# A four-layer graph network on one core: weights in order of use, a new weaving of the engines' work, and filler products on TensorE

## The reference, cut to what matters

```
L0 (twice): u = h h^T / sqrt(D); a = softmax(u) * adj; attn = a / sum(a)
            ctx = (attn*upper) (h Wl) + diag(attn) (h Ws) + (attn*lower) (h Wr); h = relu(layernorm(ctx))
L1 (twice): u = h (h Wleft)^T, h (h Wright)^T by triangle; attn = exp(u)*adj / sum
            h = relu(layernorm(attn (h Wlin)))
L2:         12 heads: softmax(q k^T * scale + 2 adj) v, then Wo
L3:         12 heads: softmax over edges (q k^T / sqrt(32) + beta adj) v
```

## Time and profile before

| | |
|---|---|
| median of three runs | 3139.33 us (3137.36 to 3139.83) |
| profiled execution | 3139.59 us, span 3137.8 us (1.8 us lie around it) |
| PE busy | 97% of the span |
| DVE, ACT, POOL busy | 83%, 67%, 12% |
| products on PE | 34944, or 546 for a graph |

### The profile page before, as it was taken

How to read it: one execution, slowest core, us unless ns; L and a number is a source line. 1 busy time by engine, 2 the same in 40 slices (tenths; PEclk the granted TensorE clock), 3 DMA queues, 4 the chain that set the end, 5 groups by cost and what they waited for, 6 DMA issues and landing times. The chain is left out here.

```text
span 3137.8 us, 87682 instructions
## 1 busy us (share of the span) xinstructions
PE 3032.1 (97%) x34944; PEld 2337.5 (74%) x34944; DVE 2606.3 (83%) x7641; ACT 2094.4 (67%) x6037; POOL 377.2 (12%) x652
## 2 busy tenths in 40 slices
PE   3899999999999999999999999999999999999986
PEld 1677777777777777777777777777777777777764
DVE  4688888888888888888888888888888888888874
ACT  4467677677677677677676676676676666666664
POOL 1111111111111111111111111111111111111100
PEclk7999999999999999999999999999999999999996
DMA  5000000000000000000000000000000000000000
GB/s 174 4 14 11 10 13 11 12 12 11 13 10 11 13 10 11 13 10 11 13 10 11 14 10 11 13 10 11 14 10 11 13 10 11 14 10 11 10 7 6
DMA packets 37904, 47.82 MB, mean 15 GB/s; under 512 B 4542, under 2 KB 37498, under 8 KB 37498
## 3 DMA queue, kind: packets, MB, share of 16 engines
q1 hardware_dynamic: 31408, 33.31, 3.4%
q10 hardware_dynamic: 6090, 8.91, 0.9%
HBM read 29.59 MB, written 12.58 MB: 13 GB/s over the span
## 5 line engine op out<-in xcount | busy, mean ns | idle before, releaser
L638 ACT ACTIVATE prob<-score,neg_head_max 128x128 f32<-128x128 f32 x1536 | 494.1, 392 | 117.5 <-DVE neg_head_max L901 117.2
L284 PE MATMUL bank_c<-htc_hi,w_hi 128*128 128x128 f16 x2304 | 397.2, 220 | 0.0
L284 PE MATMUL bank_c<-htc_lo,w_hi 128*128 128x128 f16 x2304 | 397.1, 219 | 0.0
L284 PE MATMUL bank_c<-htc_hi,w_lo 128*128 128x128 f16 x2304 | 397.0, 219 | 0.0
L284 PE MATMUL bank_a<-w_hi,hta_hi 128*128 128x384 f16 x1152 | 379.6, 330 | 0.0
L284 PE MATMUL bank_a<-w_lo,hta_hi 128*128 128x384 f16 x1152 | 378.8, 329 | 0.0
L699 DVE SCALAR_TENSOR_TENSOR pt_lo<-bank_c,pt_hi 128x384 f16<-128x384 f32 x512 | 271.1, 550 | 74.3 <-ACT pt_hi L518 70.1
L896 DVE SCALAR_TENSOR_TENSOR score<-bank_c,bias 128x384 f32<-128x384 f32 x512 | 281.0, 549 | 33.7 <-PE bank_c L459 29.8
L901 DVE TENSOR_REDUCE neg_head_max<-score 128x3 f32<-128x384 f32 x512 | 280.4, 548 | 6.8
L518 ACT ACTIVATE pt_hi<-bank_c 128x384 f16<-128x384 f32 x512 | 233.0, 481 | 63.5 <-PE bank_c L328 63.5
L328 PE MATMUL bank_c<-ident,prob 128*128 128x128 f32 x1536 | 257.8, 278 | 14.1 <-ACT prob L638 13.7
(11 more groups left out here) (200 smaller groups left out, 9183.0 us busy)
## 6 DMA issues: line engine op xcount, KB each, us to landing
x_in<-x SPq DMA_DIRECT2D x64, 192.0 KB, 2.4
out<-y_out SPq DMA_DIRECT2D x64, 192.0 KB, 1.9
w_stage<-w_t ACTq DMA_DIRECT2D x8, 576.0 KB, 3.9
adj_in<-adj SPq DMA_DIRECT2D x64, 64.0 KB, 2.1
score<-w_t ACTq DMA_DIRECT2D x4, 576.0 KB, 4.0
prob<-w_t ACTq DMA_DIRECT2D x3, 576.0 KB, 4.0
norms<-norm_rows SPq DMA_DIRECT2D x8, 192.0 KB, 6.3
w_stage<-w_t SPq DMA_DIRECT2D x2, 576.0 KB, 6.3
```

The lines of the kernel that those rows point to most:

```text
L284: mm = nc.tensor.matmul(out_ap, a, b, start=first and i == 0, stop=last and i == len(pairs_of) - 1)
L638: ex = nc.scalar.activation(prob[:, j, c, :], score[:, j, c, :], ACT.Exp, bias=neg_head_max[:, j, c:c + 1])
```

## The change

1. The order of the weights on the host, and with it W_INDEX's inner order, follows their use: L0 left, right, self (before: left, self, right); L2 v, q, k, Wo; L3 v, q, k. `weights` is called for each weight where it is first used, and no longer for a later one of the layer at once.
2. ACT and DVE split no weight ahead of the weaving; all 19 splits stand in SPLITS, which has new places. ACT issues no load of weights and of `bias_hl` any more: SP does, in one written order, with the wait for DVE's split on SP. The norms come in between, the first two early; `qk_bias` is loaded after all weights, ahead of `load(2)`.
3. POOL sets `bias_hl` to zero after the masks.
4. ORDER and FIRST are new for every engine. Each string holds each letter as often as before. Most of the difference is where the period is cut; beside it steps change places with neighbours: on PE `c12` now stands between `w2` and `w3`, with `w4` behind `x0` and only two steps x (before four, a2 and w4) between it and `c13`.
5. PE runs filler products of `ones2` with itself, 128x128, into c3 or a1 (`idle`): 110 ahead of its first step, 211 at eleven places of periods 0 to 2 (WARM_FIRST), and 500 at 37 places of the last three periods (WARM_LAST), which count from the period `graphs`. The results are not used.

The diff, without the renaming on the host, the moved `weights` calls of L1, and the semaphore declarations:

```diff
@@ -13,28 +13,40 @@
 MASKED = -9.0e15
 W_INDEX = (0, 3, 6, 9, 12, 16)
 W_STAGES = 4
-W_FIRST = 3
 
 
 ORDER = {
-    "pe": "yyybacbwwwwcwacwcbacxxcccxcxxxcxayybxxwwcabyybyyyyyydbwcwxxxxaxwcxcacxccwcccxbcxyyyyya",
-    "act": "ccxaqcbacwcwncppcpbpbwpbammmxbmcwibiiacniccbnjjjwcbcpccpppbwjncb",
-    "dve": "abcabccbcbcabccbcaapzppbpzazpabapabapaaaapbbpibxbcabibbiabbabcjbamcccjcccajaccbappppbapaaa"
-           "abncbbanqcpbax",
-    "pool": "qacmabbnab",
+    "pe": "xyyybyaybyayywcwwwbwcacwcacccxxccxxxcxxyyabxxawbcwbyyyyyyyydbwcwxwxxcxxacxxwcccacccbxc",
+    "act": "cnbxcbaccawccwcppcpbpwnbpbqammmbxmibiciawcinccbjnjjwccpbccpppbwj",
+    "dve": "nbacaccaccncczcapapazppzbpabapabaapabapbipbbxabcibibbbacbmjbcccccajcaccabjqapapppbapababaa"
+           "cbbaxbcabpbabb",
+    "pool": "babqnacamb",
 }
 FIRST = {
-    "pe": {"a": (0, 3), "b": (1, 6), "c": (2, 20), "d": (1, 0), "w": (0, 6), "x": (1, 9), "y": (2, 13)},
-    "act": {"a": (1, 2), "b": (2, 6), "c": (3, 15), "i": (2, 0), "j": (3, 0), "m": (4, 0), "n": (0, 1), "p": (4, 0), "q": (4, 0), "w": (1, 3), "x": (3, 0)},
-    "dve": {"a": (1, 13), "b": (2, 19), "c": (3, 18), "i": (2, 0), "j": (3, 0), "m": (2, 0), "n": (0, 0), "p": (4, 0), "q": (3, 0), "x": (2, 1), "z": (4, 0)},
-    "pool": {"a": (1, 2), "b": (2, 2), "c": (4, 0), "m": (2, 0), "n": (0, 0), "q": (3, 0)},
+    "pe": {"a": (0, 4), "b": (1, 6), "c": (2, 20), "d": (1, 0), "w": (0, 6), "x": (1, 10), "y": (3, 0)},
+    "act": {"a": (1, 2), "b": (2, 7), "c": (4, 0), "i": (2, 0), "j": (3, 0), "m": (4, 0), "n": (0, 2), "p": (4, 0), "q": (3, 0), "w": (1, 3), "x": (3, 0)},
+    "dve": {"a": (0, 12), "b": (1, 14), "c": (2, 18), "i": (1, 0), "j": (2, 0), "m": (1, 0), "n": (0, 0), "p": (3, 0), "q": (2, 0), "x": (1, 1), "z": (3, 0)},
+    "pool": {"a": (1, 0), "b": (2, 1), "c": (3, 0), "m": (1, 0), "n": (0, 0), "q": (2, 0)},
 }
 
 SPLITS = {
-    "act": [(1, 39), (1, 48), (1, 48), (1, 61), (1, 61), (2, 3), (2, 7), (2, 9),
-            (2, 21), (2, 24), (2, 24), (2, 24), (2, 37), (2, 43), (2, 48), (2, 50)],
-    "dve": [(1, 59), (1, 64), (1, 79), (1, 87), (1, 92), (1, 97), (2, 0), (2, 17),
-            (2, 29), (2, 33), (2, 40), (2, 45), (2, 52), (2, 59), (2, 65), (2, 79)],
+    "act": [(1, 1), (1, 1), (1, 27), (1, 27), (1, 40), (1, 51), (1, 62), (1, 62),
+            (2, 1), (2, 6), (2, 10), (2, 13), (2, 13), (2, 22), (2, 27), (2, 27), (2, 42), (2, 46), (2, 48)],
+    "dve": [(0, 0), (0, 10), (0, 45), (0, 65), (0, 68), (0, 77), (0, 84), (0, 93),
+            (0, 97), (1, 2), (1, 10), (1, 17), (1, 19), (1, 40), (1, 40), (1, 50), (1, 57), (1, 59), (1, 65)],
+}
+
+WARM_START = 110
+WARM_FIRST = {
+    (0, 41): 9, (0, 65): 5, (0, 79): 58, (1, 6): 14, (1, 25): 19, (1, 41): 15, (1, 59): 40, (2, 0): 11,
+    (2, 4): 5, (2, 41): 13, (2, 59): 22,
+}
+WARM_LAST = {
+    (0, 44): 21, (0, 48): 8, (0, 60): 9, (0, 67): 13, (0, 76): 7, (0, 78): 5, (1, 12): 9, (1, 18): 22,
+    (1, 20): 9, (1, 22): 9, (1, 24): 19, (1, 44): 21, (1, 48): 7, (1, 58): 15, (1, 62): 26, (1, 68): 9,
+    (1, 72): 13, (1, 76): 7, (1, 78): 5, (1, 82): 14, (1, 85): 9, (2, 12): 9, (2, 14): 26, (2, 20): 9,
+    (2, 22): 9, (2, 24): 19, (2, 28): 5, (2, 32): 17, (2, 36): 9, (2, 40): 56, (2, 48): 9, (2, 58): 15,
+    (2, 62): 26, (2, 68): 9, (2, 72): 13, (2, 76): 7, (2, 78): 5,
 }
 
 
...
@@ -224,11 +236,13 @@
         b_rows = self_part[0:N_W + 1, :]
         b_hi, b_lo = (of[0:N_W + 1, 0, :, :].rearrange("p c n -> p (c n)") for of in (pt_hi, pt_lo))
 
-        def woven(engine, splits=None, **streams):
+        def woven(engine, splits=None, idle=None, **streams):
 
             order, first = ORDER[engine], FIRST[engine]
             assert set(order) == set(streams), (engine, set(order) ^ set(streams))
             live, period = set(streams), 0
+            for _ in range(SPLITS.get(engine, []).count((0, -1))):
+                next(splits)
             while live:
                 seen = dict.fromkeys(streams, 0)
                 for place, letter in enumerate(order):
...
@@ -238,6 +252,8 @@
                     seen[letter] += 1
                     for _ in range(SPLITS.get(engine, []).count((period, place))):
                         next(splits)
+                    if engine == "pe":
+                        idle(WARM_FIRST.get((period, place), 0), WARM_LAST.get((period - graphs, place), 0))
                 period += 1
 
         @block.sync
...
@@ -256,18 +272,41 @@
                 sp.wait_ge(*y_ready.at(g))
                 sp.dma_start(out[g:g + 1, :, :].rearrange("a p d -> (a p) d"), y_out[g % 2][:, :]).then_inc(y_stored[g], 16)
 
+            def load_weight(m):
+                if m >= W_STAGES:
+                    sp.wait_ge(w_lo_split, m - W_STAGES + 1)
+                sp.dma_start(w_stage[m % W_STAGES], w_t[m, :, :].rearrange("(c p) n -> p c n", p=128))\
+                    .then_inc(w_loaded[m % W_STAGES], 16)
+
+            def load_norms(first, last):
+                for i in range(first, last):
+                    sp.dma_start(norms[:, i, :], norm_rows[i:i + 1, :].to_broadcast([128, D]))\
+                        .then_inc(norms0_loaded if i < 2 else norms_loaded, 16)
+
             load(0)
+            for m in range(W_STAGES):
+                load_weight(m)
             load(1)
+            load_norms(0, 2)
+            sp.wait_ge(bias_zeroed, 1)
+            sp.wait_ge(b_hi_split, 1)
+            sp.dma_start(bias_hl[0:1, :, :], b_hi).then_inc(b_spread, 16)
+            sp.wait_ge(b_lo_split, 1)
+            sp.dma_start(bias_hl[1:2, :, :], b_lo).then_inc(b_spread, 16)
+            load_weight(4)
+            load_norms(2, 4)
+            load_weight(5)
+            load_weight(6)
+            load_norms(4, 8)
+            load_weight(7)
             sp.dma_start(beta_col[:, :], beta[0:1, :].to_broadcast([128, 1])).then_inc(beta_loaded, 16)
-            for m in range(W_STAGES):
-                sp.dma_start(w_stage[m], w_t[m, :, :].rearrange("(c p) n -> p c n", p=128)).then_inc(w_loaded[m], 16)
+            for m in range(8, N_W):
+                load_weight(m)
             for i in range(2):
-                m = W_INDEX[5] + i
+                m = W_INDEX[5] + 1 + i
                 for c in range(CHUNKS):
                     sp.dma_start(qk_bias[:, i, c:c + 1], biases[m:m + 1, c * 128:(c + 1) * 128].rearrange("a p -> p a"))\
                         .then_inc(qk_bias_loaded, 16)
-            for i in range(8):
-                sp.dma_start(norms[:, i, :], norm_rows[i:i + 1, :].to_broadcast([128, D])).then_inc(norms_loaded, 16)
             for g in range(2, graphs):
                 load(g)
                 if g >= 4:
...
@@ -372,16 +411,17 @@
                     yield
                     rows_rest(a0, m, hta_hi, hta_lo, None).then_inc(hl_done[g], 1)
                     yield
+                    weights(g, l, 1)
+                    pe.wait_ge(*expo_a_ready.at(g, k))
+                    rows_first(a1, m + 1, hta_hi)
+                    yield
+                    rows_rest(a1, m + 1, hta_hi, hta_lo, None).then_inc(hr_done[g], 1)
+                    yield
+                    pe.wait_ge(*hl_ready.at(g, k))
                     weights(g, l, 2)
-                    pe.wait_ge(*expo_a_ready.at(g, k))
-                    rows_first(a1, m + 2, hta_hi)
-                    yield
-                    rows_rest(a1, m + 2, hta_hi, hta_lo, None).then_inc(hr_done[g], 1)
-                    yield
-                    pe.wait_ge(*hl_ready.at(g, k))
-                    rows_first(a0, m + 1, hta_hi)
-                    yield
-                    rows_rest(a0, m + 1, hta_hi, hta_lo, None).then_inc(hs_done[g], 1)
+                    rows_first(a0, m + 2, hta_hi)
+                    yield
+                    rows_rest(a0, m + 2, hta_hi, hta_lo, None).then_inc(hs_done[g], 1)
                     yield
 
             def turn_adj(g):
...
@@ -486,13 +527,14 @@
             def weight_c(g):
                 for l in range(2):
                     k, m = l + 1, W_INDEX[4 + l]
-                    weights(g, 4 + l, 3 - l)
+                    weights(g, 4 + l, 0)
                     pe.wait_ge(*htc_hi_ready.at(g, k))
-                    rows_first(c1, m + 2, htc_hi)
-                    yield
-                    rows_rest(c1, m + 2, htc_hi, htc_lo, htc_lo_ready.at(g, k)).then_inc(v_done[g], 1)
-                    yield
-                    for bank, of, done in (c2, 0, q_done), (c3, 1, k_done):
+                    rows_first(c1, m, htc_hi)
+                    yield
+                    rows_rest(c1, m, htc_hi, htc_lo, htc_lo_ready.at(g, k)).then_inc(v_done[g], 1)
+                    yield
+                    for bank, of, done in (c2, 1, q_done), (c3, 2, k_done):
+                        weights(g, 4 + l, of)
                         for o in range(CHUNKS):
                             mm = columns(bank, m + of, htc_hi, htc_lo, o)
                             if o == CHUNKS - 1:
...
@@ -509,7 +552,18 @@
                 for g in range(graphs):
```

(60 more changed lines are left out.)

## The result

The changed kernel took 3049.53 us (median of 4 runs, 3048.86 to 3050.41), the kernel before 3138.57 beside it (3137.36 to 3139.83): a ratio of 0.9716 [0.9700, 0.9733], 89 us faster. I had said 3101 us, with a range of 3083 to 3125.

What follows compares the result with a forecast made beforehand. PE was taken to run at its own rate in the middle, so only the ends could win: 3139.6 less 25 (head), 14 (tail) and 0 (middle) gave 3100.6, put at 3101 us, range 3083 to 3125.

Steps and rivals of the forecast that it cites:

- start, splits and the new wait: Three head terms: 8.6 us won at the start, 15 on weight splits, 3.5 lost waiting for graph 2's load.
- filler in the head: Idle products on PE in the first periods raise its clock: 5 us won, from a loss of 2 to 9.
- the tail: Last periods: filler keeps PE's clock up, 14 us won, of 20.8 at most.
- The middle, priced: Steady periods between the ends: 0 change; ends a gain of 0.19 us per graph or a loss of 0.25.
- the floor: Lowest time per graph in the middle: 46.94 us less some 0.2, the idle time that PE shows.
- The splits: Weight splits on ACT and DVE, decoupled by SP's loads and waits: 15 us won, between 5.7 and 26.
- The start: Before graph 0's first transposes: `a0.0` at about 11.1 us instead of 19.73, 8.6 us won, 7 to 9.
- The new wait: Graph 2's load behind all weights and `qk_bias` in SP's queue, issued about 48.5 us: cost 3.5 us, 0 to 5.
- B: Rival: new wait every period at `c12` to `c13`, transposes waiting for `prob`; 3149 us at 0.8 us per graph; chance 0.09.
- C: Rival "more than I take": decoupling gives its 26 us and the tail 18, total 3085 us; chance 0.09.
- A: Rival: the ends give half, from late loads or filler not holding the clock; 3112 to 3128 us; chance 0.18.
- D: Rival: nothing happens, the head's gain is given back; 3139 us or so; chance 0.04.

Runs made afterwards that it cites:

- e3: New orders and split places, with the loads, norms and POOL memset of the kernel before and no filler: 3075.91 us, ratio 0.981.
- e1: The changed kernel without any filler products: 3059.54 us, ratio 0.9758.
- e2: New loads, weight and norm order and POOL memset place, with the orders, first places and split places of before, no filler: 3130.57 us, ratio 0.9982.
- e4: The kernel before plus four useless 128-column products per graph ahead of `c11`, the `node_c` transposes in L3: 3135.36 us, ratio 0.9999.
- e5: The kernel before plus twelve useless 128-column products per graph ahead of `c11`: 3155.16 us, ratio 1.0062.
- e6: The kernel before plus four useless products per graph ahead of the q products of L3, where nothing waits: 3152.99 us, ratio 1.0054.
- e9: e1 plus four useless 128-column products per graph ahead of `c11`: 3072.28 us, ratio 0.9795.
- e12: The changed kernel with graph 2's load issued ahead of the last weight and of `qk_bias`: 3046.14 us, ratio 0.9711.
- e10: e3 with PE's order and first places of before, so only ACT, DVE and POOL follow new orders: 3413.93 us, ratio 1.0882.

## Why the prediction was wrong, point by point

| step of the prediction | forecast, us | measured in the spans, us |
|---|---|---|
| start, splits and the new wait | -20.1 | -15.5 with the new orders (e3 to e1), -8.6 with the old (e2) |
| the new orders in the head | 0, not priced | -19.9 (before to e3) |
| filler in the head | -5 | -0.7 (e1 to the changed kernel) |
| the middle | 0 | -40.0 |
| the tail | -14 | -13.6: orders -4.7, loads -1.2, filler -7.7 |

Of the 51 us by which the forecast missed, 40 are the middle and 11 the head (36.1 where the sum had 25).

**The step that failed is "The middle, priced", and in it the floor: "46.94 us less some 0.2".** I took the idle time that PE's records show, 0.2 us per graph, for all that a better order could win, and read "97% busy" as PE at its own rate. The earlier trace rows does not even show that idle time: it has one wait of 0.4 us for `node_c`, where the timeline has a gap of 0.12 at the place in every graph. The lateness of PE's products was 1.4 us per graph, 0.285 of it at the very `node_c` that stands in the earlier trace rows, and its records covered all but 0.2. The order took back 0.667 us of it, 40 us in all. e3 shows that the orders did it, e4, e5, e6 and e9 that the hidden wait at `c11` is real, has that size and is used up in the new order. For the other five places the lateness is read from starts, for two of them from PEld's waits too; they were not tested one by one.

**The head's orders.** This is a second term, put at nothing without a reason: I priced what the new SP queue and the exchange would give, and not what a new order of the steps gives to a chain of waits. 19.9 of the 36.1 us are that.

**The splits.** I took 15 us for the decoupling, from ends of 5.7 and 26. With the old orders it gave 3 us (the head's 8.6 less 5.4 at `a0.0`), under the lower end; with the new ones 10.9 (15.5 less 4.6), and these are net of the new wait. With the 3.3 us that e12 won back in the head they are 14.2, so with the new orders the term was right in size. In the medians the new loads, start included, gave 5.5 us with the old orders and 16.4 with the new ones (e3 to e1), where the issues that ACT was spared come to 5.7. The Trainium skill, DMA: Bandwidth & Descriptors, "Issuing engines are not separate DMA queues", says that starting DMAs from more engines saves only the sequencer's time for issuing them. With the old orders the measurement does not go beyond that. With the new ones it does, by 10.7 us. My reading is that waits were moved along with the issues, and that there they stood on the chain; the order of the loads and POOL's memset moved in the same step, and no run parts them.

**Right.** The start (10.66 against 11.1 us). The new wait: `x_in` of graph 2 issued at 47.42 where I had said 48.5, PE waiting 3.0 us, and 4.6 us won by e12 (3.3 in the head's mark) where I had 3.5, of 0 to 5. The tail's sum of 14 us came out by luck: all 14 were to be the filler's, which gave 7.7, and the rest came with the orders and loads. Of the 20.8 us that I had counted as the most, 14 was too large a part; that the rest of what filler speeds up stands beside waits on ACT and DVE is likely but not shown. The Trainium skill, TensorE: Matmul & The Clock Gate, "Part 1: The HAM clock gate", puts the penalty of the ramp under 1% of a typical kernel's span. What the filler gave back here, 10 us, is 0.3% of the span and in line with that.

**The rivals.** B did not happen: in the middle of the changed kernel PE waits for no `prob`. e10 shows the size it can have when orders don't fit (81.9 us). C, "more than I take", had the right sign and the wrong place; it allowed nothing for the middle and so stopped at 3085. A and D did not happen. The range was too narrow because its one bound on the middle, 0.19 us per graph, came from the same reading as the floor.

## What to carry to other kernels

- Before calling an engine bound by its own rate, compare starts with the distances that the same shapes keep where nothing holds them, and read the waits of the weight load beside those of the product. A wait that comes as often as there are periods names a place to look at, even if no idle time is shown; what it costs is read from the starts.
- A suspected hidden wait is tested cheaply: put useless work of its length exactly there. If it costs nothing, the wait is real, and an order that fills or removes it can gain that much.
- The orders of engines with in-order queues are one design; with the new ones on three engines and the old one on PE the kernel took 3413.93 us, against 3137.58 before and, with the same old loads and no filler, 3075.91 with all four new (e3). Price a new order by what each step waits for, not by the count of its products. And in an in-order DMA queue, put the load that a chain needs next ahead of small ones with long issues: six `qk_bias` columns took 2.86 us to issue.

## What the runs showed of the hardware

- If PE is held up by up to about 0.17 us, no idle time shows between the records of f16 products with 128 or 384 columns (records of 0.22 and 0.33 us, distances of 0.056 and 0.163).
- A product held by a semaphore starts 0.05 to 0.06 us after the end of the work that it waits for (1001.77 after 1001.72, 1002.90 after 1002.84), and the one behind it is late by a further 0.055 us.
- The score products over 32 rows (L459 before, L500 after) begin 0.09 us later than the product before them would let a full-height one begin, in both kernels; at one of the four places (two in each kernel) it was 0.17.
